# Fill by rows with a short first wait, unread products in the drain, the embedding's variance on ScalarE, one gate operation, and an end done tile by tile

## The chip, the cores and the metric

The kernel runs on one core of a Trainium2 chip. The metric is the device time of one execution in microseconds; lower is better. A core has TensorE (PE, matrix products into PSUM), VectorE (DVE), ScalarE (ACT), GpSimd (POOL) and SyncE (SP, which here only issues DMAs), each with its own instruction stream; they meet in semaphores. The profile shows TensorE's granted clock as a share of 2.4 GHz; its other level here is 1.2 GHz.

## What is computed

A small vision tower on 128 images of 64 x 64 x 3, in fp32. Patches of 16 x 16 give 16 tokens an image, 2,048 tokens of width 128.

```python
xs = concat([x, right, left, down, up])          # the image and four shifts by a pixel
y = conv(xs, conv_w, stride 16) + conv_b         # (2048 tokens, 128)
y = (y - mean(y)) * rsqrt(var(y) + 1e-3) * gamma + beta
h = y @ dense_w + dense_b
# attention without softmax, 8 heads of 16, causal decay within an image
a = layernorm(h)
scores = (q @ k.T / 4) * gammas[h] ** (j - i)    # 0 where j < i
h = h + silu(a @ wg.T + bg) * (scores @ v)
# experts: 64, top 2 of sigmoid logits, capacity 256 rows each
z = layernorm(h)
top_scores, top_idx = top_k(sigmoid(z @ gate_w.T), 2)   # weights normalised, times 2.5
routed = sum_k weight_k * (silu(rows @ w1[e]) * (rows @ w3[e])) @ w2[e]
h = h + (silu(z @ sw1) * (z @ sw3)) @ sw2 + routed
```

## The kernel before

The 2,048 tokens are 16 tiles of 128 (`NT`), in four convolution groups of four tiles (`NG`, `TG`).

**Token stage** (the loop `for i in range(LAST)` with 21 passes, written once for each engine). It is a software pipeline over tiles. Pass i of TensorE runs, in this order: a convolution product `conv_step(i, 0)`, `attend(i-3)`, `embed(i+1)`, `places(i-5)`, `scores(i-2)`, `turn(i)`, `conv_step(i, 1)`, `logits(i-4)`, `project(i-1)`. The convolution of group g+1 is spread over the passes of group g, two products of 512 columns a pass; from pass 11 on there is none left, and from pass 15 on no `embed`. I call the passes from 11 on the drain. fp32 products show as two instructions each in the profile.

DVE's pass: `decay_scores(i-3)`, `choose(i-5)`, `embedded(i)`, `gated(i-3)`, `y_stats(i+1)`, `attended(i-3)`, `accumulate(i-5)`, `place(i-5)`. `y_stats` (L798) takes mean and variance of an embedded tile, which `embed` (L423) has transposed into PSUM bank `A`; `gated` (L831) multiplies attention's output by the gate, in two operations of 64 partitions, because the two halves of the tokens lie in two PSUM banks.

ScalarE's pass: `norm_h2(i-4)`, `norm_h(i-1)`, `evac_turned(i)`, `tanhs(i-4)`, now and then `evac_y`, `evac_qk(i-1)`, `evac_vg(i-1)`. GpSimd's pass: `rstd(i)` (L1041), which gives the reciprocal deviations of three tiles that stand at different points of the pipeline, and then `send(i-6, k)` for k = 0, 1 (L1062), an indirect DMA that scatters the tile's 128 rows to the row buffer of their experts. GpSimd works in order: while a `send` waits, the next `rstd` does.

**Expert rows.** The buffer `buf` in HBM holds 256 rows (`CAP`) for each of 64 experts, then spare rows for overflow and a block of dropped rows. It has to be zero before tokens are scattered into it. `fill` is a zeroed SBUF tile of 128 partitions and 16 rows of 512 bytes (`FILLR`). SP writes it out in 8 DMAs of 1 MB (`FILLS`): the buffer is seen as 128 stretches of 128 rows, one a partition, so that each DMA writes 16 rows of each stretch, and an expert is complete only after all eight. `send(0, 0)` waits for all of them (L1067).

**SP's queue in that stage** (L298 to L347): the loads of groups 0 and 1 with the constants, a wait for the four parts of group 1 (`x_in`, L319), the drop rows, the first fill, the load of group 2 (three parts of X at 0.5 MB, one of XE at 0.38 MB that covers 96 partitions), seven more fills, the load of group 3, two fills of spare rows, then the experts' weights, paced by `y_ps`. A load of group g >= 2 waits until group g-2 has been convolved.

**Expert stage** (L599): 17 rounds of four experts: rows in by SP, four transposes, products with w1 and w3, silu on ScalarE, products on DVE, `down`, result to `buf`. It starts when all scatters have landed (L377). **Shared expert and end:** TensorE, ScalarE and DVE compute the shared expert in 8 parts; GpSimd gathers two rows a token with 32 indirect DMAs (L1097); DVE adds them to `h`, weighted, in 8 pairs of tiles (L1005): two operations for the first choice, a wait, two for the second; SP stores each pair (L397).

## Time and profile before

| | |
|---|---|
| median of 3 runs | 237.4 us (235.38 to 239.8) |
| the profiled execution | 236.28 us, of which the span of the instructions is 234.5 |
| mean granted clock of TensorE | 0.842 |
| busy: PE, DVE, POOL, ACT | 163.5, 135.6, 107.2, 83.7 us |
| DMA | 42.96 MB, 183 GB/s on average |
| chain that ended last | PE 32%, DMA 21%, POOL 14%, issue 10%, DVE 8% |

Times in the profile count from the first instruction. The chain of work that ended last is followed back from the last instruction, at each step to what released it. Its largest entry by line is GpSimd's gathers, L1097, 12%; then the DMA of the fills, 10%. The share of an engine over the whole span says little here, since the stages have different limits; each part of the change has to be read in its own stage.

### The profile page before, as it was taken

The numbers are of one execution on the slowest core, as the hardware profiler recorded it, in microseconds if no ns is written. First come the engines' busy times: TensorE is split into PE (matmuls) and PEld (weight loads), VectorE is DVE, ScalarE is ACT, GpSimd is POOL, SyncE is SP. The second block draws the span as 40 slices with busy tenths as digits, with TensorE's granted clock in tenths as the row PEclk, the third lists the DMA queues.
The fourth block names the chain that finished last, engine by engine and source line by source line (L and its number), as shares of the span: only waits on it lengthen the run. The fifth ranks groups of instructions, "written<-read, shape, count | busy, mean of one in ns | idle before, by whom it ended". The sixth has DMA issues, their size and how long they took to land.

```text
span 234.5 us, 4462 instructions
## 1 busy us (share of the span) xinstructions
PE 163.5 (70%) x1402; PEld 113.3 (48%) x1402; DVE 135.6 (58%) x487; ACT 83.7 (36%) x229; POOL 107.2 (46%) x169
## 2 busy tenths in 40 slices
PE   0888899997999987888988305999998655530000
PEld 0334455664666655656575204888887433320000
DVE  1525646684768898886447781577777422229222
ACT  2010565555256676653552202555554101100000
POOL 4004322225836666675446750133330077777760
PEclk9999999999599999975555555999999999995555
DMA  6999799999998744300000118699742612224421
GB/s 245 390 315 291 231 379 422 425 414 361 389 289 227 225 141 130 117 22 25 22 22 15 35 45 246 170 257 286 249 121 81 192 41 55 56 52 121 118 73 34
DMA packets 29213, 42.96 MB, mean 183 GB/s; under 512 B 2752, under 2 KB 21376, under 8 KB 27904
## 3 DMA queue, kind: packets, MB, share of 16 engines
q1 hardware_dynamic: 26176, 35.27, 45.0%
q0 software_dynamic: 3008, 7.34, 10.6%
q8 instruction: 13, 0.21, 0.4%
q14 instruction: 16, 0.13, 0.2%
HBM read 24.45 MB, written 18.15 MB: 182 GB/s over the span
## 4 chain that ended last, share of the span: by engine, by line
PE 32%; DMA 21%; POOL 14%; issue 10%; DVE 8%; SPq 8%; ACT 3%; POOLq 1%; DVEq 0%; ACTq 0%
POOL X L1097 12%; DMA expert_rows<-EW 10%; DMA XE<-xe 6%; PE bank L583 5%; PE scores L484 5%; PE bank L575 4%; PE scores L473 3%; PE conv_counts L419 3%; DVE go L837 2%; SPq L307 2%; DMA expert_rows<-ys 2%; PE bank L459 2%; PE bank L507 2%; POOL expert_rows L1069 2%; PE scores L596 2%
## 5 line engine op out<-in xcount | busy, mean ns | idle before, releaser
L1097 POOL DMA_INDIRECT X<-expert_rows,slots x32 | 30.6, 956 | 21.8 <-DMA expert_rows<-ys 12.3
L1069 POOL DMA_INDIRECT expert_rows<-xrow,slots x32 | 32.4, 1013 | 14.6 <-issue 8.3
L419 PE MATMUL conv_counts<-X,W 128*128 128x512 f32 x48 | 26.9, 666 | 8.0 <-DVE W L776 6.6
L688 ACT ACTIVATE qm<-bank,bqm,C 128x128 f32<-128x128 f32 x64 | 24.1, 460 | 7.0 <-PE bank L452 7.0
L484 PEld LDWEIGHTS scores<-vg,ST 64*64 64x64 f32 x512 | 19.4, 156 | 10.2 <-issue 10.2
L973 DVE TENSOR_TENSOR hT<-bank,gs 64x256 f32<-64x256 f32 x34 | 14.5, 427 | 15.1 <-ACT gs L745 14.7
L1085 POOL DMA_DIRECT2D expert_rows<-ys x12 | 9.1, 762 | 27.5 <-DVE ys L987 27.5
L484 PE MATMUL scores<-vg,ST 64*64 64x16 f32 x512 | 20.9, 222 | 0.7 <-DVE ST L884 0.2
L1054 POOL TENSOR_TENSOR VE<-MV,EPS 128x3 f32<-128x3 f32 x20 | 4.0, 199 | 36.6 <-issue 15.2
L1055 POOL TENSOR_TENSOR RS<-VE,mhalf 128x3 f32<-128x3 f32 x20 | 17.8, 889 | 1.6
L837 DVE TENSOR_TENSOR go<-scores,vg 64x128 f32<-64x128 f32 x32 | 9.1, 286 | 15.3 <-PE scores L484 15.1
L583 PE MATMUL bank<-xbT,EW 128*128 128x128 f32 x128 | 17.9, 285 | 0.0
L737 ACT ACTIVATE xbT<-bank 128x512 f32<-128x512 f32 x17 | 10.2, 597 | 20.5 <-PE bank L575 20.5
L575 PE MATMUL bank<-C,xb 128*128 128x128 f32 x68 | 11.7, 302 | 7.4 <-DMA xb<-expert_rows 7.4
L661 ACT ACTIVATE xT<-bank 128x256 f32<-128x256 f32 (+1 forms) x19 | 6.7, 351 | 28.0 <-PE bank L444 22.6
L583 PEld LDWEIGHTS bank<-xbT,EW 128*128 128x128 f32 x128 | 16.4, 200 | 0.4 <-issue 0.3
L1010 DVE SCALAR_TENSOR_TENSOR h<-X,pw,h 128x128 f32<-128x128 f32 x32 | 9.5, 349 | 11.7 <-DMA X<-expert_rows,slots 9.6
L419 PEld LDWEIGHTS conv_counts<-X,W 128*128 128x128 f32 x48 | 8.6, 212 | 15.1 <-DMA X<-xp 11.4
L473 PE MATMUL scores<-qm,kT 64*64 64x256 f32 x128 | 12.5, 462 | 4.6 <-DVE go L837 4.5
L745 ACT ACTIVATE gs<-bank 64x512 f32<-64x512 f32 x17 | 10.0, 589 | 6.7 <-PE bank L583 6.6
L575 PEld LDWEIGHTS bank<-C,xb 128*128 128x128 f32 x68 | 7.8, 150 | 9.4 <-DMA xb<-expert_rows 7.6
L1058 POOL TENSOR_SCALAR NM<-MV,RS 128x1 f32<-128x1 f32 x40 | 10.3, 271 | 4.2 <-POOL RS L1055 4.2
(129 smaller groups left out, 338.1 us busy)
## 6 DMA issues: line engine op xcount, KB each, us to landing
expert_rows<-EW SPq DMA_DIRECT2D x10, 1024.0 KB, 17.8
X<-xp SPq DMA_DIRECT2D x12, 512.0 KB, 10.8
xb<-expert_rows SPq DMA_DIRECT2D x16, 256.0 KB, 4.1
expert_rows<-ys POOLq DMA_DIRECT2D x12, 256.0 KB, 3.3
EW<-w SPq DMA_DIRECT2D x4, 512.0 KB, 4.3
EW<-wp SPq DMA_DIRECT2D x3, 640.0 KB, 6.4
XE<-xe SPq DMA_DIRECT2D x4, 384.0 KB, 13.0
expert_rows<-ys SPq DMA_DIRECT2D x4, 256.0 KB, 3.0
```

What stands on the lines that cost most here:

```text
L419: mm = nc.tensor.matmul(CONV[:, :], w, x, start=(j == 0), stop=(j == NCH + 1))
L473: mm = nc.tensor.matmul(S[toks, n, 0:QM * TB], kT[rows, t % 2, toks], qm[rows, t % 2, :, toks], start=True, stop=True)
L484: mm = nc.tensor.matmul(S[toks, c, AVC + hh * HD:AVC + (hh + 1) * HD], ST[toks, t % 2, hh], vg[toks, t % 4, hh * HD:(hh + 1) * HD], start= ...
L575: mm = nc.tensor.transpose(XT[u][:, e * BLK:(e + 1) * BLK], xb[:, v, e], ident)
L583: mm = nc.tensor.matmul(GU[u][:, e * BLK:(e + 1) * BLK], w[:, e], xbT[:, u, e], start=True, stop=True)
L688: nc.scalar.activation(qm[:, t % 2, m], QK[:, 0:P], ACT.Identity, bias=bqm[:, m:m + 1], scale=head[:, m:m + 1])
L837: ins = nc.vector.tensor_tensor(go[toks], S[toks, c, AVC:AVC + P], vg[toks, t % 4, P:2 * P], ALU.mult)
L973: ins = nc.vector.tensor_tensor(hT[a * HID:(a + 1) * HID, u], up[:, a], gate[:, a], ALU.mult)
L1055: own(pool.tensor_tensor(RS[:, b], VE[:, :], mhalf[:, :], ALU.pow))
L1058: ins = pool.tensor_scalar(NM[:, b, k:k + 1], MV[:, b, k, 0:1], RS[:, b, k:k + 1], -1.0, ALU.mult, ALU.mult)
L1069: pool.indirect_dma_start(buf, bass.IndirectOffsetOnAxis(ap=slots[:, k, t:t + 1], axis=0), xrow[:, t % XR], None).then_inc(sent[t % XR], 16)
L1097: pool.indirect_dma_start(pr[:, t, k], None, buf, bass.IndirectOffsetOnAxis(ap=slots[:, k, t:t + 1], axis=0)).then_inc(pr_in[t // TS], 16)
```

## The change

It has six parts.

1. **Fills by rows.** The buffer is now seen as 64 experts of 256 rows. A fill writes 16 rows of every expert from 64 partitions of `fill`, the lower and the upper half in turn: 16 DMAs of 0.5 MB. After eight of them the first 128 rows of every expert are zero, and more than that the first tile cannot reach. `send(0, 0)` waits for those eight, `send(1, 0)` for the rest (`filled_rest`). Group 2 is loaded after two fills (as many bytes as before). SP waits for the first two parts of group 1 only.
2. **Unread products.** Where a convolution product stood, the drain gets one of 256 columns that nobody reads, `idle_product`: two a pass from pass 11, three from pass 16, and 12 (`TURNOVER`) after the last count.
3. **Variance on ScalarE.** `embed` multiplies by `center` (the identity less 1/128) in place of transposing, so that the tile arrives without its mean; ScalarE squares it and sums (`y_variance`). DVE's `y_stats` is gone.
4. **One gate operation.** Both halves of `attend` write to the same PSUM bank, on different partitions, and `gated` is one operation of 128 partitions.
5. **End by tiles.** DVE adds a tile's two rows in two dependent operations, tile after tile; SP stores pairs, but the last two tiles one by one.
6. The semaphores that go with these (`pr_in` for each tile).

```diff
-        FILLS = NE * CAP // P // FILLR
+        FILLS = CAP // FILLR
+        FIRST_FILLS = P // FILLR
+        TURNOVER = 12
@@ sync
-            for part in range(NL + 1):
+            for part in range(NL - 1):
                 sp.wait_ge(x_in[1][part], 16)
-            main = buf[0:NE * CAP].rearrange("(p r) w -> p r w", p=P)
+            main = buf[0:NE * CAP].rearrange("(e r) w -> e r w", e=NE)
             for n in range(FILLS):
-                if n == 1:
+                if n == 2:
                     load_group(2)
-                sp.dma_start(main[:, n * FILLR:(n + 1) * FILLR], fill[:, :, :]).then_inc(filled, 16)
+                half = slice(n % 2 * NE, (n % 2 + 1) * NE)
+                sp.dma_start(main[:, n * FILLR:(n + 1) * FILLR], fill[half]
+                             ).then_inc(filled if n < FIRST_FILLS else filled_rest, 16)
@@ sync, the stores
-            for p in range(NS):
-                sp.wait_ge(fin_ready, p + 1)
-                sp.dma_start(ov[:, p * TS:(p + 1) * TS], h[:, p * TS:(p + 1) * TS]).then_inc(stored, 16)
+            ends = list(range(TS, NT, TS)) + list(range(NT - TS + 1, NT + 1))
+            for first, end in zip([0] + ends, ends):
+                sp.wait_ge(fin_ready, end)
+                sp.dma_start(ov[:, first:end], h[:, first:end]).then_inc(stored, 16)
@@ tensor
-                nc.tensor.transpose(A[:, 0:P], y, ident)
+                nc.tensor.matmul(A[:, 0:P], y, center, start=True, stop=True)
-                        mm = nc.tensor.matmul(S[toks, c, AVC + hh * HD:AVC + (hh + 1) * HD], ST[toks, t % 2, hh],
+                        mm = nc.tensor.matmul(S[toks, 0, AVC + hh * HD:AVC + (hh + 1) * HD], ST[toks, t % 2, hh],
+            def idle_product(i, n):
+                if i == NT - TG - 1 and n == 0:
+                    pe.wait_ge(yT_ready, NG)
+                nc.tensor.matmul(CONV[:, 0:2 * P], W[:, 0], W[:, 1:3], start=True, stop=True)
             def conv_step(i, n):
                 g, j = (i + 1) // TG + 1, 2 * ((i + 1) % TG) + n
+                if g >= NG:
+                    return idle_product(i, n)
@@ tensor, in the loop, after places(i - 5), and after the last count
+                if i >= NT:
+                    idle_product(i, 2)
+            for n in range(TURNOVER):
+                idle_product(LAST, n)
@@ scalar
+            def y_variance(t):
+                act.wait_ge(y_ps, t + 1)
+                nc.scalar.activation(ysq[:, :], A[:, 0:P], ACT.Square, scale=P ** -0.5,
+                                     accum_out=MV[:, t % 2, 0, 1:2]).then_inc(ystat, 1)
                 if 0 <= i - 1 < NT:
                     norm_h(i - 1)
+                if i + 1 < NT:
+                    y_variance(i + 1)
@@ vector
-                for c in range(NTB):
-                    toks = slice(c * TB, (c + 1) * TB)
-                    ins = nc.vector.tensor_tensor(go[toks], S[toks, c, AVC:AVC + P], vg[toks, t % 4, P:2 * P], ALU.mult)
-                ins.then_inc(av_read, 1)
+                nc.vector.tensor_tensor(go[:, :], S[:, 0, AVC:AVC + P], vg[:, t % 4, P:2 * P], ALU.mult
+                                        ).then_inc(av_read, 1)
-                if i + 1 < NT:
-                    y_stats(i + 1)
+            for t in range(NT):
+                dve.wait_ge(pr_in[t], 16 * TOPK)
+                dve.wait_ge(so_ready, t // TS + 1)
                 for k in range(TOPK):
+                    ins = nc.vector.scalar_tensor_tensor(out=h[:, t], in0=pr[:, t, k], scalar=pw[:, t, k:k + 1],
+                                                         in1=h[:, t], op0=ALU.mult, op1=ALU.add)
                     if k < TOPK - 1:
+                        own(ins)
                 ins.then_inc(fin_ready, 1)
@@ gpsimd, send(t, k)
                 if t == 0:
-                    pool.wait_ge(filled, 16 * FILLS)
+                    pool.wait_ge(filled, 16 * FIRST_FILLS)
                     pool.wait_ge(drop_filled, 16)
+                if t == 1:
+                    pool.wait_ge(filled_rest, 16 * (FILLS - FIRST_FILLS))
```

## Rows read from the trace of the kernel before

**Rows 1.** The page's slices: granted clock of TensorE, tenths, 40 slices.

```profile
PEclk9999999999599999975555555999999999995555
```

**Rows 2.** Chain that ended last, in order of time: start, us, what.

```profile
30.91 22.66 DMA expert_rows<-EW
...
143.22 1.97 PE bank L575 x8
```

**Rows 3.** Timeline of GpSimd: start, us, line and work, idle time before.

```profile
48.69 0.51 POOL L1058 TENSOR_SCALAR NM<-MV,RS 128x1 f32<-128x1 f32 x2 [0.21 <-POOL RS L1055]
54.61 1.23 POOL L1069 DMA_INDIRECT expert_rows<-xrow,slots  x1 [5.42 <-DVE slots L863]
...
129.30 0.22 POOL L1054 TENSOR_TENSOR VE<-MV,EPS 128x3 f32<-128x3 f32 x1 [0.69 <-DVE MV L849]
```

**Rows 4.** Timeline of TensorE: attends of passes 6, 8, 11, 15, 18, and others.

```profile
49.81 1.11 PE L484 MATMUL scores<-vg,ST 64*64 64x16 f32 x32
...
54.89 1.13 PE L419 MATMUL conv_counts<-X,W 128*128 128x512 f32 x2
...
58.88 0.45 PE L429 MATMUL bank<-C,yT 128*128 128x128 f32 x1 [1.82 <-DVE h L871]
...
66.19 1.11 PE L484 MATMUL scores<-vg,ST 64*64 64x16 f32 x32
...
76.27 0.60 PE L459 MATMUL bank<-SQ,xT 128*128 128x256 f32 x2
76.70 0.27 PE L460 MATMUL bank<-bvg,ones 96*128 96x256 bf16 x1
...
82.78 1.11 PE L484 MATMUL scores<-vg,ST 64*64 64x16 f32 x32
...
105.15 1.89 PE L484 MATMUL scores<-vg,ST 64*64 64x16 f32 x32
...
125.76 1.89 PE L484 MATMUL scores<-vg,ST 64*64 64x16 f32 x32 [0.24 <-DVE ST L884]
...
135.55 0.27 PE L567 MATMUL conv_counts<-acc,ones 128*128 128x64 bf16 x2 [0.47 <-DVE mpos L856]
```

**Rows 5.** Busy time by stretch, clock, DMA share, GB/s: XE loads; fills alone.

```profile
20.50:22.50 2.00, 2.00 (x8) 1.02 (x7) 1.65 (x7) 0.00 (x0) 0.72 (x4) 1.00 1.01 209
31.90:33.40 1.50, 1.50 (x24) 0.74 (x24) 0.00 (x0) 1.50 (x7) 0.00 (x0) 1.00 0.89 273
36.00:50.00 14.00, 13.52 (x137) 8.61 (x137) 9.81 (x39) 8.43 (x27) 4.77 (x12) 1.00 1.01 423
55.50:57.00 1.50, 1.50 (x34) 1.01 (x32) 0.00 (x0) 1.09 (x5) 1.20 (x2) 1.00 1.09 243
```

**Rows 6.** The same for two drain steps: length, PE, PEld, DVE, ACT, POOL, clock.

```profile
88.10:93.43 5.33, 4.26 (x58) 3.08 (x59) 4.80 (x22) 3.47 (x12) 3.61 (x7) 1.00 0.44 133
105.10:112.65 7.55, 6.62 (x56) 4.58 (x55) 4.45 (x19) 3.47 (x12) 4.53 (x8) 0.50 0.09 27
```

**Rows 7.** Timeline of DVE: gate and y_stats in a drain step; the end.

```profile
84.28 0.57 DVE L837 TENSOR_TENSOR go<-scores,vg 64x128 f32<-64x128 f32 x2
84.88 0.30 DVE L803 BATCH_NORM_STATS2 stats<-bank 128x6 f32<-128x128 f32 x1
85.21 0.18 DVE L805 BATCH_NORM_AGGREGATE MV<-stats 128x2 f32<-128x6 f32 x1
...
229.44 1.26 DVE L1010 SCALAR_TENSOR_TENSOR h<-X,pw,h 128x128 f32<-128x128 f32 x4 [3.57 <-DMA X<-expert_rows,slots]
```

**Rows 8.** Timeline of ScalarE in a drain step.

```profile
91.40 0.38 ACT L661 ACTIVATE xT<-bank 128x256 f32<-128x256 f32 x1 [1.06 <-PE bank L444]
```

**Rows 9.** Issue to landing: fill 0 (24.32), XE of group 2 (27.36), X of group 3 (31.44).

```profile
DMA to landing us min/median/max: 5.1/5.1/5.1
...
DMA to landing us min/median/max: 7.7/7.7/7.7
...
DMA to landing us min/median/max: 23.4/24.7/26.2
```

More of the change, by code:

```diff
@@ L168, in tower @@
         go = sb("go", [P, P])
+        ysq = sb("ysq", [P, P])
         xrow = sb("xrow", [P, XR, P])
@@ L225, in tower @@
         filled_tile, filled = sem("filled_tile"), sem("filled")
-        spare_filled, drop_filled = sem("spare_filled"), sem("drop_filled")
+        filled_rest, spare_filled, drop_filled = sem("filled_rest"), sem("spare_filled"), sem("drop_filled")
         ones_set = sem("ones_set")
@@ L252, in tower @@
             "sh_ps", "shg_ready", "shT_ready", "so_ps", "so_ready"))
-        pr_in = [sem(f"pr_in{n}") for n in range(NS)]
+        pr_in = [sem(f"pr_in{n}") for n in range(NT)]
         fin_ready, stored = sem("fin_ready"), sem("stored")
@@ L287, in turns @@
             return min(max(i - FIRST2 + 1, 0), LAST2 - FIRST2 + 1)
-        FILLS = NE * CAP // P // FILLR
+        FILLS = CAP // FILLR
+        FIRST_FILLS = P // FILLR
         SPARES = NOV * BLK // P // FILLR
         PACE = 6
-        assert FILLS * FILLR * P == NE * CAP and SPARES * FILLR * P == NOV * BLK
+        TURNOVER = 12
+        assert FILLS * FILLR == CAP and SPARES * FILLR * P == NOV * BLK
         def first_blocks(g):
@@ L340, in load_weights @@
                 sp.wait_ge(w_ready, NL)
-                sp.wait_ge(filled, 16 * FILLS)
+                sp.wait_ge(filled, 16 * FIRST_FILLS)
+                sp.wait_ge(filled_rest, 16 * (FILLS - FIRST_FILLS))
                 sp.wait_ge(spare_filled, 16 * SPARES)
@@ L396, in _ @@
             ov = out.rearrange("(t p) d -> p t d", p=P)
-            for p in range(NS):
-                sp.wait_ge(fin_ready, p + 1)
-                sp.dma_start(ov[:, p * TS:(p + 1) * TS], h[:, p * TS:(p + 1) * TS]).then_inc(stored, 16)
-            sp.wait_ge(stored, 16 * NS)
+            ends = list(range(TS, NT, TS)) + list(range(NT - TS + 1, NT + 1))
+            for first, end in zip([0] + ends, ends):
+                sp.wait_ge(fin_ready, end)
+                sp.dma_start(ov[:, first:end], h[:, first:end]).then_inc(stored, 16)
+            sp.wait_ge(stored, 16 * len(ends))
         @block.tensor
@@ L717, in _ @@
             nc.scalar.activation(WD[:, :], QK[:, 0:P], ACT.Copy).then_inc(wd_ready, 1)
+            y_variance(0)
             for i in range(LAST):
@@ L796, in step @@
                 return steps[0]
-            def y_stats(t):
-                dve.wait_ge(y_ps, t + 1)
-                if t == 0:
-                    dve.wait_ge(ones_set, 1)
-                s = step(nc.vector.bn_stats(stats[:, 0], A[:, 0:P]))
-                dve.wait_ge(dve_step, s)
-                nc.vector.bn_aggr(MV[:, t % 2, 0], stats[:, 0]).then_inc(ystat, 1)
             def choose(t):
@@ L909, in split_bias @@
                 ins.then_inc(bvg_ready, 1)
-            y_stats(0)
             for i in range(LAST):
@@ L1003, in _ @@
                     evac_out(n + NB, 0)
-            for p in range(NS):
-                dve.wait_ge(pr_in[p], 16 * TOPK * TS)
-                dve.wait_ge(so_ready, p + 1)
+            for t in range(NT):
+                dve.wait_ge(pr_in[t], 16 * TOPK)
+                dve.wait_ge(so_ready, t // TS + 1)
                 for k in range(TOPK):
-                    for t in range(p * TS, (p + 1) * TS):
-                        ins = nc.vector.scalar_tensor_tensor(out=h[:, t], in0=pr[:, t, k], scalar=pw[:, t, k:k + 1],
-                                                             in1=h[:, t], op0=ALU.mult, op1=ALU.add)
-                        if k < TOPK - 1:
-                            last = step(ins)
+                    ins = nc.vector.scalar_tensor_tensor(out=h[:, t], in0=pr[:, t, k], scalar=pw[:, t, k:k + 1],
+                                                         in1=h[:, t], op0=ALU.mult, op1=ALU.add)
                     if k < TOPK - 1:
-                        dve.wait_ge(dve_step, last)
+                        own(ins)
                 ins.then_inc(fin_ready, 1)
@@ L1098, in _ @@
                         pr[:, t, k], None, buf,
-                        bass.IndirectOffsetOnAxis(ap=slots[:, k, t:t + 1], axis=0)).then_inc(pr_in[t // TS], 16)
+                        bass.IndirectOffsetOnAxis(ap=slots[:, k, t:t + 1], axis=0)).then_inc(pr_in[t], 16)
 def kernel(x, L0_tok_conv_w, L0_tok_conv_b, L0_tok_gamma, L0_tok_beta, L0_tok_dense_w, L0_tok_dense_b,
```

3 lines of the change are left out of this document (1 added, 2 removed).

## The prediction

> **What bounds the kernel now.** I read the page first, then the chain that ended last, then the timelines of the engines on it. The slices show the granted clock of TensorE: a slice is 5.86 us, and it is full up to the 10th, half in the 11th (from 58.6), full again, and half from the 19th to the 25th (105.5 to 146.6) [rows 1]. So three things are to be placed: a stall near 55 us, a slow drain of the token stage from about 100 us on, and the end. Step i of the token stage means pass i of its loop; I know a pass by its `attend`, the 32 small products of L484.
>
> The chain passes through one long DMA: the last fill of the expert rows, issued at 30.91 and landed 22.66 us later, at 53.6 [rows 2]. GpSimd's first scatter waits for it: GpSimd was done with its statistics at 49.2 and starts the scatter at 54.61 [rows 3]. It issues in order, so the next `rstd` is late, DVE's `embedded` with it, and TensorE starts the embedding of step 7 only at 58.88; the attend of step 8 starts at 66.19 [rows 4]. Later, over the four steps from 82.78 to 105.15, a step costs 5.6 us, over the three from 105.15 to 125.76 it is 6.9 [rows 4]. In one step of the first stretch DVE is busy 4.80 of 5.33 us and TensorE 4.26; in one of the second TensorE, at half clock, is busy 6.62 of 7.55 and DVE only 4.45 [rows 6]. So DVE bounds the drain at 2.4 GHz and TensorE at 1.2 GHz. The clock fell some 20 us after the last convolution product (which lies before the attend at 82.78), in steps in which the engine was busy 80% of the time. After that: the expert stage (TensorE starts on the rows that have landed at 143.22 [rows 2]), and gathers on GpSimd with one DVE group of four behind the last [rows 7].
>
> **Fills.** Before, 8 DMAs of 1 MB read all 128 partitions of `fill`; after, 16 of 0.5 MB read 64 each, the two halves in turn. Bytes are the same, 8.39 MB. All SP loads go through one queue and land in order, so what counts is the whole queue: drop rows, fills, group 2, fills, group 3. Three dates come from rows. Fill 0 landed at 29.4 (24.32 + 5.1) and XE of group 2 at 35.1 (27.36 + 7.7), so group 2 takes 5.7 us. The first X part of group 3 landed at 54.85 (31.44 + 23.4), 1.3 after the last fill [rows 9]. TensorE starts the first product on it at 54.89 [rows 4]: this data is just in time, and it stays behind all the fills. SP no longer waits for the last two parts of group 1, so the queue runs on without the gap in which SP issued: I let the fills begin at 23.7. Group 3's first part then lands at 23.7 + 8.39 MB / rate + 5.7 + 1.3.
>
> The rate is the unknown that decides. Between 36 and 50 us, fills alone, the queue moved 423 GB/s at a DMA share of 1.01. But while the XE load of group 1, 2 or 3, which covers 96 partitions, is in transit, the share stays near one and the bytes fall: 209, 273 and 243 GB/s [rows 5]. The engines are then busy and yet slow, so a transfer over fewer partitions is slower in this trace. No row shows 64 partitions in bulk. Lower bound 209, upper bound 423; the mean of the three XE stretches is 242, and 64 is further down than 96, so I take the middle between that and 209, 225 GB/s. Then the fills take 37.3 us and group 3 begins to land at 68.0.
>
> The Trainium skill bears on this. "SBUF — State Buffer", section on the DMA port swizzle, says that partitions 0 to 63 reach only 8 of the 16 ports, about 218 GB/s instead of 436, and that two DMAs in flight, one on each half, were only 6% quicker than one. By it the fills take 38.5 us and the sum below comes to 238.7; by the row of 423 GB/s it comes to 220.3. The rule speaks against the change, and the three XE rows agree with its direction.
>
> What waits then? The first wait, for 8 of the 16 fills (4.2 MB, 18.6 us, plus group 2), ends at about 48.4, before GpSimd is free at 49.2: it is hidden. The new wait of scatter 1 for the rest ends at about 67. Behind it on GpSimd stand `rstd(8)`, then `embedded(8)`, and all of the next step. TensorE waits meanwhile itself, for X of group 3. After 68.0 it does that product (1.7 at half clock: 512 columns, four times the 0.43 found below for 256) and the attend (1.9), so the embedding of step 7 starts at about 71.7 and the attend of step 8 some 6.8 later, at 78.5 (before: 7.3 later, six of them at half clock). Against 66.19 that is **+12.3 us**. The 8 more issues on SP (0.46 each) lie in its waits; the weight loads behind them are not used before 143. If the fills run at 423, the data lands at 50.5, the stall goes and with it its price. That price: the attends of steps 6 and 8 lie 16.38 apart, and two undisturbed steps take 2 x 5.8 (the three from 66.19 to 82.78, 16.59, plus the 0.86 of convolution that the last of them lacks), so **4.7 us**.
>
> **Drain.** Per step DVE loses `y_stats` (0.30 + 0.18) and one of the two gate operations (0.57 for two, so 0.29) [rows 7]: about 0.7. TensorE gets two products of 256 columns; one such pair takes 0.43, from 76.27 to 76.70 [rows 4]. It also gets a second pass for `center` (0.06). 4.26 + 0.86 + 0.06 is 5.2: TensorE becomes the bound, the step goes from 5.6 to 5.15 on average, **-1.8** over four. The variance on ScalarE stands where that engine idles 1.06 before L661 [rows 8]. A 128-column activation with a sum isn't in the trace; it costs between nothing and that row's 0.38 for 256 columns and twice that, all of it under the idle time. The wait of the first product for the last `evac_y` is met by then.
>
> With the fillers TensorE is busy nearly all of a step, as it was while the convolution ran and the clock stayed full. So I let it hold 2.4 GHz. The three steps from 105.15 then cost 3.3 (half of 6.62) + 0.9 to 1.3 of fillers; GpSimd and DVE allow no less than about 4.5 [rows 6], so 4.5 + 4.8 + 4.5 against 20.6: **-6.8**. From the last attend to the `rstd` that starts GpSimd's closing run it is 3.5 now (125.76 to 129.30 [rows 3]) and 2.3 with a 1.1 us attend: **-1.2**. The run itself is scatters and keeps its length. The 12 closing products take 5.1 us behind the last count (135.55 now [rows 4]), 7.7 before the rows are there, so they end some 2.5 early; whether the clock is still full then is open: between 0 and 1.5 (the first eight transposes take 1.97 at half clock [rows 2], a product group as much after them), I take **-0.7**.
>
> **End.** After the last gather DVE runs four operations in 1.26 [rows 7]; after, two dependent ones, 0.73. The last store is 64 KB instead of 128: **-0.6** together, bounds 0.4 and 0.9. One more store costs SP half a microsecond before the last data is there.
>
> **Sum.** +12.3 - 1.8 - 6.8 - 1.2 - 0.7 - 0.6 = +1.2. The profiled execution took 236.28 (span 234.5 and 1.8 around it), so 237.5. The median of the three runs is 237.4, between 235.38 and 239.8: no change.
>
> **Rivals.** (1) The fills keep 423 GB/s because the halves alternate and the engines drift apart: -4.7 - 11.1 - 0.2 for an earlier start gives 220.3. For it: ordinary fills never slow down after 36 us, and the XE penalty varies (209 to 273). Against it: at 20.5 every engine was slow at once. Above 258 GB/s the result is faster by over 2%. (2) Slower: the clock is not held. Then each filler costs 0.86 instead of 0.43. The three steps take 8.4, 9.3 and 7.0 (+4.1), the tail +1, and twelve closing products need 10.3 where 7.7 are free (+2.6); with the rest, +5.3 in place of -11.1, so 254. It decides once half of the drain runs at 1.2 GHz. For it: the clock fell at 80% busy; against: the fillers close just those gaps. (3) The fills run below 200 GB/s, more than two engines on one port: each 10 GB/s less costs 2 us; at 170 it is 249. (4) The drain is bound by the chain through ScalarE and GpSimd and gives half: 242.
>
> **Chances.** Forecast 0.50 (its own range 232 to 243), (1) 0.30, (2) 0.08, (3) 0.07, (4) 0.05. Within 2% (about what a measurement of this kernel can tell): 0.42 of the forecast and 0.03 of (4), 0.45. Faster: (1) and 0.04 of the forecast, 0.34. Slower: (2), (3), 0.02 of (4), 0.04 of the forecast, 0.21. The range must take in (1), so 218 to 243; it leaves out (2), most of (3) and little else.
>
> **What would show it.** The stretch 36 to 60 near 225 GB/s with the DMA share at one; the 16th fill landing near 67; GpSimd waiting some 12 us before its third scatter; TensorE waiting as long at L419 for X; the attend of step 8 near 78; from there no half clock; steps of 5.2 and then 4.5 to 4.8; DVE idle in the drain. Wrong it is if the 36 to 50 stretch still moves over 400, or if slices of half clock remain in the drain.

## The result and the profile after

The changed kernel took 223.37 us (median of four runs, 222.13 to 224.05) against 236.59 of the kernel before on the same chip (235.38 to 239.8): ratio 0.945, 95% interval 0.938 to 0.953. It is faster; the forecast was 237.5 and no change. Of the profiled execution the span is 220.3 us, before 234.5.

On the chips of the experiments the kernel before took 226 to 242 us, at a mean granted clock from 0.91 down to 0.81. Its one trace (0.842) has the half clock in the drain; that it is this stretch which differs from execution to execution is likely, but only that one trace was kept. So most of what follows compares intervals within traces. The ratios to before in the sections below are taken among executions within some 1.5% of the fastest of each kernel, so they can differ from the quotient of the medians.

The slices of the changed kernel (clock and what the DMA engines moved) stand beside [rows 1]: the stall in the 11th slice and the half clock of the drain are gone.

```profile
PEclk9999999999999999999999997999999999985555
DMA  6999999999999984510000168799534412124530
```

The stretch of fills alone as in [rows 5], and one drain step as in [rows 6] (length, PE, PEld, DVE, ACT, POOL, clock, DMA share, GB/s):

```profile
36.00:50.00 14.00, 14.00 (x158) 9.26 (x156) 8.38 (x33) 9.70 (x34) 5.37 (x12) 1.00 1.01 419
88.59:93.74 5.15, 5.11 (x64) 3.76 (x63) 4.25 (x19) 3.73 (x14) 3.61 (x7) 1.00 0.46 130
```

The fills alone, 64 partitions each, moved 419 GB/s where 225 was forecast; over 400 in this stretch was the prediction's own sign of being wrong. Timeline of GpSimd, as [rows 3]: its first scatter now starts at 48.56 (54.61 before), behind its own work and no fill, and the `rstd` that starts its closing run at 116.25 (129.30).

```profile
48.56 1.23 POOL L1081 DMA_INDIRECT expert_rows<-xrow,slots  x1 [0.52 <-issue]
...
54.05 1.07 POOL L1081 DMA_INDIRECT expert_rows<-xrow,slots  x1 [0.29 <-issue]
...
116.25 0.21 POOL L1064 TENSOR_TENSOR VE<-MV,EPS 128x3 f32<-128x3 f32 x1
```

Timeline of TensorE, as [rows 4]: the attends of passes 6, 8, 11, 15 and 18, the product on X of group 3 between the first two, and the idle products behind the count.

```profile
49.27 1.11 PE L491 MATMUL scores<-vg,ST 64*64 64x16 f32 x32
54.80 1.12 PE L426 MATMUL conv_counts<-X,W 128*128 128x512 f32 x2 [0.62 <-DMA X<-xp]
...
61.54 1.11 PE L491 MATMUL scores<-vg,ST 64*64 64x16 f32 x32
...
78.31 1.11 PE L491 MATMUL scores<-vg,ST 64*64 64x16 f32 x32
...
98.89 1.11 PE L491 MATMUL scores<-vg,ST 64*64 64x16 f32 x32
...
113.25 1.11 PE L491 MATMUL scores<-vg,ST 64*64 64x16 f32 x32 [0.31 <-DVE ST L900]
...
122.40 5.43 PE L548 MATMUL conv_counts<-W 128*128 128x256 f32 x24
130.14 0.66 PE L593 MATMUL bank<-C,xb 128*128 128x128 f32 x4 [2.32 <-DMA xb<-expert_rows]
```

Stage by stage, from attend to attend of the passes named, the change of the span comes out whole:

| stretch | before | after | change | forecast |
|---|---|---|---|---|
| start to attend of pass 8 | 66.19 | 61.54 | -4.65 | +12.3 |
| to pass 11 | 16.59 | 16.77 | +0.18 | 0 |
| four steps, to pass 15 | 22.37 | 20.58 | -1.79 | -1.8 |
| three steps, to pass 18 | 20.61 | 14.36 | -6.25 | -6.8 |
| to the `rstd` that starts the closing run | 3.54 | 3.00 | -0.54 | -1.2 |
| to the first gather | 58.60 | 57.66 | -0.94 | -0.7 |
| to the last gather | 39.09 | 38.88 | -0.21 | 0 |
| to the end of the span | 7.48 | 7.48 | 0.00 | -0.6 |

### The profile page after: what moved, and what is told of

It is laid out like the page before. It is cut to its first block, busy times and chain, and to the rows that moved or that the text cites. A ratio compares the mean times of both kernels' runs of the same rounds, so it can differ in the third digit from the quotient of the medians.

```text
span 220.3 us, 4641 instructions
## 1 busy us (share of the span) xinstructions
PE 168.2 (76%) x1492; PEld 118.2 (54%) x1492; DVE 125.6 (57%) x439; ACT 88.8 (40%) x261; POOL 106.6 (48%) x169
## 4 chain that ended last, share of the span: by engine, by line
PE 42%; POOL 16%; DMA 16%; SPq 13%; issue 9%; DVE 1%; POOLq 1%; ACT 0%; DVEq 0%
POOL X L1109 13%; DMA X<-xp 11%; PE bank L601 8%; SPq L332 7%; PE scores L491 5%; PE bank L593 4%; PE conv_counts L426 3%; PE conv_counts L548 3%; SPq L310 3%; PE scores L480 3%; PE scores L614 3%; PE conv_counts L614 2%; PE bank L466 2%; POOL expert_rows L1081 2%; PE bank L436 2%
## 5 line engine op out<-in xcount | busy, mean ns | idle before, releaser
L491 PEld LDWEIGHTS scores<-vg,ST 64*64 64x64 f32 x512 | 16.2, 134 | 9.1 <-issue 8.3
L548 PE MATMUL conv_counts<-W 128*128 128x256 f32 x74 | 20.7, 390 | 0.0
L764 ACT ACTIVATE xbT<-bank 128x512 f32<-128x512 f32 x17 | 10.2, 597 | 20.1 <-PE bank L593 20.1
L491 PE MATMUL scores<-vg,ST 64*64 64x16 f32 x512 | 17.7, 207 | 0.3 <-DVE ST L900 0.3
L1022 DVE SCALAR_TENSOR_TENSOR h<-X,pw,h 128x128 f32<-128x128 f32 x32 | 10.3, 351 | 9.5 <-DMA X<-expert_rows,slots 6.7
L853 DVE TENSOR_TENSOR go<-scores,vg 128x128 f32<-128x128 f32 x16 | 4.7, 292 | 15.2 <-PE scores L491 15.2
L548 PEld LDWEIGHTS conv_counts<-W 128*128 128x128 f32 x74 | 12.2, 192 | 1.6 <-ACT yT L662 0.2
L734 ACT ACTIVATE shg<-conv_counts 128x256 f32<-128x256 f32 x8 | 3.1, 384 | 23.7 <-PE conv_counts L525 23.7
L900 DVE TENSOR_TENSOR ST<-scores,C 128x512 f32<-128x512 f32 x16 | 11.1, 692 | 1.9 <-PE scores L480 1.9
## 6 DMA issues: line engine op xcount, KB each, us to landing
X<-xp SPq DMA_DIRECT2D x12, 512.0 KB, 10.5
```

What stands on the lines that cost most here:

```text
L491: mm = nc.tensor.matmul(S[toks, 0, AVC + hh * HD:AVC + (hh + 1) * HD], ST[toks, t % 2, hh], vg[toks, t % 4, hh * HD:(hh + 1) * HD], start= ...
L548: nc.tensor.matmul(CONV[:, 0:2 * P], W[:, 0], W[:, 1:3], start=True, stop=True)
L900: nc.vector.tensor_tensor(ST[:, t % 2].rearrange("p (n m) i -> p n (m i)", m=QM), S[:, :, 0:QM * TB], decay.rearrange("p (n f) -> p n f", ...
```

## The fills: which partitions, which order, which wait

**e1_lower_half.** All fills read the same 64 partitions.

```
-                half = slice(n % 2 * NE, (n % 2 + 1) * NE)
+                half = slice(0, NE)
```

> The changed kernel with one edit: all 16 fills read partitions 0 to 63 of the zero tile; before this edit they took the lower and the upper half in turn. Bytes, rows written and number of transfers stay. Theory A (64 partitions are slow by themselves, and only the alternation of halves, with several transfers in flight, hid it): the fills move about 218 GB/s, 38 us instead of 20, the first X part of group 3 lands near 69 instead of 54.8, TensorE waits some 14 us for it, and the time is about 223.4 + 15 = 238. Theory B (how many partitions a fill reads does not matter for its rate): over 400 GB/s between 36 and 50, X at 54.8, time 223 to 224.

**e2_half_blocks.** `half = slice(n // 8 * NE, (n // 8 + 1) * NE)`.

> The changed kernel with one edit: the first eight fills read partitions 0 to 63, the last eight partitions 64 to 127, so neighbours in the queue read the same half. Theory A: as slow as with the lower half alone, 236 to 238, since only the two fills at the change of halves overlap. Theory B: 223 to 224, over 400 GB/s.

Measured: 242.57 us (242.21 to 243.85) and 242.97 (241.59 to 243.87), some 5 us more than either theory A expected; ratio to before on that chip 1.072 for both (the medians, 232.27 before, give 1.04 and 1.05). The unedited changed kernel took 222.5 on that chip. The windows of the first, then of the second (columns as above):

```profile
42.00:50.00 8.00, 8.00 (x86) 5.24 (x84) 5.81 (x25) 5.70 (x19) 3.27 (x8) 1.00 1.00 208
57.00:66.00 9.00, 0.00 (x0) 0.00 (x0) 0.00 (x0) 0.11 (x1) 0.00 (x0) 0.63 1.00 213
```

```profile
42.00:50.00 8.00, 8.00 (x90) 5.24 (x91) 5.80 (x25) 5.86 (x21) 3.29 (x7) 1.00 0.99 221
57.00:66.00 9.00, 0.00 (x0) 0.00 (x0) 0.00 (x0) 0.00 (x0) 0.00 (x0) 0.55 0.98 222
```

Theory A holds. Fills of 64 partitions run at half the rate, 208 to 222 GB/s, with the DMA share still at one, when their neighbours in the queue read the same half; with the halves in turn they run at 419. In the trace's packet records an 8 KB packet takes 636 to 638 ns (medians) in the first case and 309 in the second. In e1 X of group 3 lands at 70.85 (expected 69), TensorE stands still from 54.6 to 70.9, and the clock is half from 59.4 to 79.9, so that the attend of pass 8 comes at 81.78, 20.2 us later than in the changed kernel. That half clock, under which TensorE works for the last 9 us of it, was in neither theory and fits the 5 us on top.

**e3_old_fills.** The fills, the waits for them and SP's full wait as before, all else as changed. Of its edit, the line of the fill:

```
-                sp.dma_start(main[:, n * FILLR:(n + 1) * FILLR], fill[half]
-                             ).then_inc(filled if n < FIRST_FILLS else filled_rest, 16)
+                sp.dma_start(main[:, n * FILLR:(n + 1) * FILLR], fill[:, :, :]).then_inc(filled, 16)
```

> The changed kernel with the fills as before: 8 transfers of 1 MB from all 128 partitions, the scatter of the first tile waits for all of them, and SP waits for all four parts of group 1 first. Everything else stays. If the hidden first wait is worth what the stall cost before (4.7 us between the attends of passes 6 and 8), the attend of pass 8 is again near 66.2 and the time is 223.4 + 4.7 = 228. If TensorE's wait for X of group 3 had been the true end of that stall, no more than 1 us: 224.

**e11_long_first_wait.** The fills stay, the first scatter waits for all of them.

```
                 if t == 0:
                     pool.wait_ge(filled, 16 * FIRST_FILLS)
+                    pool.wait_ge(filled_rest, 16 * (FILLS - FIRST_FILLS))
```

> The changed kernel, but the first scatter waits for all 16 fills, not for the first eight. The fills stay by rows, half a tile each, in the same order. Theory (the short first wait is what removes the stall; earlier issue and smaller transfers bring nothing): scatter 0 at 54 instead of 48.6, attend of pass 8 near 66 with the clock at half behind it, 223 + 4.7 = 227.5, as with the old fills. Rival (the earlier start of the fills has a part in it): 224 to 226.

Measured: 228.01 (226.46 to 228.77) with the old fills, as expected; scatter 0 at 54.81, attend of pass 8 at 66.61. With the long first wait alone 226.79 (224.97 to 229.87; the unedited changed kernel did not run on that chip), scatter 0 at 53.88, the clock half for 3.4 us where it was half for 6.8, and the attend of pass 8 at 64.28, where 66 was expected. Against 61.54 the old fills cost 5.07 us up to that attend, the long first wait alone 2.74. So the short first wait is more than half of what takes the stall away. The other 2.3 us go with a first scatter 0.9 earlier and the shorter stretch at half clock; whether other executions divide alike no trace shows.

**e7_full_wait.** `range(NL - 1)` is `range(NL + 1)` again, so SP starts the fills later.

> The changed kernel with SP's wait for all four parts of group 1 ahead of the fills again, so that they start 3 us later, as before (23.9 instead of 20.9). Everything behind stays. In the trace of the changed kernel X of group 3 landed at 54.75, where it landed before (54.85), so the earlier start seems to have been lost between 20.5 and 28, where 222 to 234 GB/s were moved. Theory (the earlier start brings nothing): X of group 3 lands within 0.7 us of 54.8 and the time is that of the changed kernel, 222 to 229. Rival (it brings its 3 us): X lands near 57.5, TensorE waits 3 us, the clock falls at 57, and no execution is under 226.

Measured: 232.46 (226.07 to 233.82); before on that chip 232.02 (the unedited changed kernel did not run there, v2 of the next section took 223.25). My theory fell and the rival holds. The fills were issued from 23.12, 1.8 us later than in the changed kernel, X of group 3 landed at 56.4, and TensorE waited for it:

```profile
56.41 1.80 PE L426 MATMUL conv_counts<-X,W 128*128 128x512 f32 x2 [2.07 <-DMA X<-xp]
```

The clock fell at 56.7 for 6.8 us, and the attend of pass 8 came at 66.23. The halves in turn have a price at the start of the queue. Windows of the kernel before and of the changed one:

```profile
25.00:28.00 3.00, 2.88 (x15) 1.96 (x16) 1.42 (x6) 1.18 (x4) 1.43 (x4) 1.00 1.00 318
```

```profile
25.00:28.00 3.00, 3.00 (x17) 2.00 (x16) 0.85 (x4) 1.82 (x7) 1.56 (x4) 1.00 0.97 234
```

In both the first fills are in transit there, beside loads of X. The first 1 MB of fills landed 5.1 us after its issue before and in e3; in two halves it took 6.8 in e7, which starts behind the same wait, and 7.0 in the changed kernel. By the landing of XE of group 2 the loss has grown to 2.6 to 2.9 us (10.8 us behind the issue of the first fill before, 13.4 in e7, 13.7 in the changed kernel), and in the fills that follow nothing more is lost. Why the start is slower is not shown. The earlier start, 21.28 instead of 24.32, pays for that loss, so that X of group 3 lands at 54.75 as it did before; without it every execution was 226 or more.

## When X of group 3 lands

**v2_x_ahead.** The first part of group 3 goes ahead of the last two fills (and is left out of `load_group(3)`).

```
+                if n == FILLS - 2:
+                    sp.wait_ge(conv_ps, 2)
+                    sp.dma_start(X[:, 1, 0:HC], xp[3, :, 0:HC]).then_inc(x_in[1][0], 16)
```

> The changed kernel with one edit: the first X part of group 3 is loaded ahead of the last two fills. In profiled executions of kernels with the part behind the fills TensorE waited 0.46, 0.62, 1.71, 2.33, 2.94 and 3.45 us for it, and in those with more than 1.7 the clock fell to half near 57.5 for 3.4 to 10.2 us. Theory (that wait is what makes the changed kernel differ by 8 us between executions): no wait for X at L426 above 0.3 us, no half clock near 57, all executions between 221.5 and 223.5. Rival (the clock falls there for another reason): executions near 227 to 230 remain.

Measured: 223.25 (220.1 to 224.06), all six executions within 4 us, where 2 were expected, at a mean clock of 0.934 to 0.942, and none near 227. The product no longer waits:

```profile
54.53 1.10 PE L429 MATMUL conv_counts<-X,W 128*128 128x512 f32 x2
```

There is a price: the last fill now lands at 57.69, the scatter of the second tile waits 4.3 us for it (58.49 instead of 54.05), and the attend of pass 9 comes at 67.23, as in the changed kernel (67.24). So where X had been in time the edit gains nothing there; what it takes away are the slow executions.

Most of the changed kernel's spread is probably that of this landing. Of its three profiled executions the two with waits of 0.46 and 0.62 us took 222.44 and 222.13; in the third, a2 below, 228.69, TensorE waited 2.94 us for X and the clock was half from 57.85 for 6.8. The product on X after a wait of 2.33 us (the kernel with one early product, below) is followed by an attend at half clock, 1.81 us instead of 1.11:

```profile
56.32 1.13 PE L426 MATMUL conv_counts<-X,W 128*128 128x512 f32 x2 [2.33 <-DMA X<-xp]
57.38 1.81 PE L491 MATMUL scores<-vg,ST 64*64 64x16 f32 x32
```

and the attend of pass 8 comes at 66.19 there, 4.65 us later than at 61.54. Waits of 0.46 to 1.29 in other traces had no such fall behind them, but for those of e3 (1.15) and e11 (0.76), in which the stall of the late first scatter stands close behind; one of 1.71 had one of 3.4 us.

## The drain: products, DVE, places

**e4_no_products.** No idle product anywhere (the matmul in `idle_product` is left out).

> The changed kernel without any of the idle products, in the drain and behind the count alike; variance on ScalarE, one gate operation and the fills stay. Theory of the prediction (the products hold the clock): the clock falls to half near pass 15, the three attends from pass 15 to 18 take some 20 us again instead of 14.4, the tail 1 us more, the steps before the fall 5.0 or less instead of 5.15: 223.4 + 6 to 7 = 230. Rival (DVE's relief made the drain faster and the clock would have held, or does not matter): 223 to 225.

Measured: 224.69 (220.91 to 229.0); the executions differ by 8 us. In the profiled one, 220.91, the clock held until 110.0 and was half for 23.9 us. The expected times were wrong: at full clock a step took 4.70 us, not 5.0, and the three attends from pass 15 to 18 took 13.68, not some 20, because the clock held 33 us behind the last convolution product (75.9 to 76.9), where it had held 21 in the kernel before. Slices of this execution, and its product of the logits in a step at full clock:

```profile
PEclk9999999999999999999955557999999999985555
```

```profile
90.96 0.43 PE L514 MATMUL bank<-SQ,xT 128*128 128x64 f32 x2 [0.47 <-ACT xT L684]
```

TensorE waits 0.47 us for ScalarE ahead of the logits there. So the products cost 0.44 us in a full step, 2.24 over the seven steps from pass 11 to 18 (34.94 in the changed kernel, 32.70 here). What they seem to buy is that the clock doesn't fall early: 222.5 with them (five of six within 221.5 to 224.3, one 227.68), on the same chip 220.91, 221.67, 227.72 and 229.0 without. The mean clock was 0.89 in the two short ones and 0.86 in the two long ones, of which no trace was kept. The profiled one also shows that DVE's relief alone can bring the fast drain, without any product.

**e10_one_product.** Only the product ahead of the attend (`n == 0`); **v1_late_product** only the one ahead of the logits.

```
                 if g >= NG:
-                    return idle_product(i, n)
+                    return idle_product(i, n) if n == 0 else None
```

> The changed kernel with one idle product a step in the drain instead of two (the one ahead of the attend; the one ahead of the logits is left out). Without any, a step took 4.70 us at 2.4 GHz until the clock fell at 109.99; with two it took 5.14 and the clock stayed. Theory A (one is enough to hold the clock): steps of 4.92, 7 x 0.22 = 1.5 us faster than the changed kernel, clock full to the expert stage. Theory B (it isn't): the clock falls to half between passes 15 and 18, as without any, and the time is 0 to 6 us above the changed kernel, differing from execution to execution.

> The changed kernel with one idle product a step in the drain again, but the other one: the product ahead of the attend is left out, the one ahead of the logits stays. The trace without products shows TensorE idle 0.69 us ahead of the logits (it waits there for ScalarE's copy of the transposed rows) and no idle time ahead of the attend; with one product ahead of the attend a step still took 5.14. Theory A (the product ahead of the attend is the whole price, the other one is free, and one holds the clock until the expert stage): steps of 4.70 to 4.75, 2.8 us faster than the changed kernel (222.5 on this chip), about 219.7. Theory B (a product a step is no cover): the clock falls in the drain as without any, at 110 or earlier, and the time is 221 to 229, differing from execution to execution. Theory C (any product costs its 0.22): 221.5.

Measured: e10 225.18 (222.81 to 226.08), v1 220.66 (218.94 to 223.75). With the one product ahead of the attend the seven steps from pass 11 to 18 take 34.93 us (82.96 to 117.89), as with two (34.94); neither of its theories said that. The clock held over these steps, and was half from 118.95 to 129.19. With the one ahead of the logits the seven steps take 32.68, as without any (32.70), and theory A holds for the price: the product in TensorE's wait for ScalarE is free, the one ahead of the attend is the whole 0.44. For the clock it holds only in part, in v1 it was half from 117.4 to 124.2, behind the last attend at 111.04. The unedited changed kernel did not run on v1's chip, so its 220.66 has no neighbour there.

**e8_dve_undone.** `y_stats` with its two operations and the gate in two halves are back on DVE.

> The changed kernel with DVE's part undone: the variance of the embedding is again two DVE operations (0.30 and 0.18 us) behind the transposing product, and the gate is again two operations of 64 partitions (0.57 together). Idle products, fills and end stay. Theory (with the products DVE and TensorE would both bind a drain step, DVE at 5.3 to 5.6): the eight steps of the drain take 5.5 instead of 5.14, +2.5 to 3.5 us over the changed kernel. Rival (TensorE with its products is the bound and covers 0.75 us of DVE work): less than 0.8 us slower.

Measured: 225.94 (223.72 to 227.65), on the chip where the changed kernel took 222.5. From the attend of pass 3 to that of pass 18 it took 83.16 us against 80.32: +2.8, of which 1.6 lie in the drain (steps of 5.33) and 1.3 in the steps with convolution (5.79 against 5.69). The first theory holds in size, but not in place: its steps of 5.5 were 5.33, and that DVE also binds a little while the convolution runs was not in it. In this run the clock stayed full through the whole drain, until 135.7, so the idle products hold it without DVE's relief too.

## The closing products

**e5_no_closing.** `TURNOVER = 0`; **e6_closing18** has 18.

> The changed kernel without the 12 closing products behind the count; the products of the drain stay. In the changed kernel the clock fell to half 1.8 us after the expert transposes began, for 3.4 us, and the first down product came 5.47 us after the transposes began against 5.60 before. Theory (the closing products gave nothing, 0.1 us at most): same time as the changed kernel within 0.5 us. Rival (the prediction: they let the expert stage start at full clock, 0.7): 0.7 to 1.5 us slower, because the clock falls while TensorE idles for 8 us and stays half over the first groups.

> The changed kernel with 18 closing products instead of 12. Twelve end 2.3 us before the expert rows are there, and the clock fell to half 1.8 us after the expert transposes began; from the last scatter to the first store of expert results it is 13.2 to 13.4 us, where kernels whose clock was full in that stretch took 11.7 to 11.9. Theory (the idle stretch ahead of the rows causes the fall): the clock stays full into the expert stage, 1.4 us faster than the changed kernel. Rival (the fall comes from what TensorE does in the expert stage's first groups, or the six further products delay it): same time, or 0.3 us slower.

Measured: e5 223.08 (221.9 to 224.98), with 12 of them 222.5 on that chip. From the last scatter to the first store of expert results it is 13.62 us without and 13.19 with, but from the last scatter to the first gather 49.28 without and 50.37 with. So they are worth about half a microsecond at most, between the two theories, and nearer the first. e6 took 225.79 (220.98 to 228.66), the unedited kernel 226.34 on that chip; in the profiled execution, 228.66, X of group 3 landed late (TensorE waited 3.45). Within its trace the clock stayed full from 67.5 to 204, and from the last scatter to the first gather it took 48.47 us, against 49.04 and 50.37 in two traces with twelve, which differ by more than the gain in question; to the first store 12.30 against 13.36 and 13.19. That points to a gain of 1 us; one trace doesn't show it.

Other traces bear on the rival. Where the clock was full in the first expert groups, the first down product came 4.79 (e6), 4.31 (e10) and 4.25 us (v1 and both v3) behind the first transpose, with twelve closing products in all but e6; in the traces in which the clock fell in the stage it came after 5.32 to 5.57 (changed kernel 5.47), without closing products (e5) after 5.82. So a full clock there goes with 0.7 to 1.2 us less. In e10, v1 and v3 the clock had fallen behind the drain and risen again before the expert rows landed. The twelve products of the changed kernel leave TensorE idle for 2.3 us just ahead of the stage.

## The end

**e9_end_undone.** Additions and stores by pairs of tiles again.

> The changed kernel with the end by pairs of tiles again: DVE waits for the gathers of two tiles and adds them in four operations, SP stores 128 KB at a time, eight stores. Theory of the prediction (the last tile alone is done sooner): 0.4 to 0.9 us slower than the changed kernel. Rival (nothing is gained: from the start of the last gather to the end of the span it is 7.51 us in the trace before and 7.47 in that after): same time within 0.3 us.

**x2_last_store_later.** Four operations more ahead of the last store.

```
+                if t == NT - 1:
+                    own(ins)
+                    for _ in range(3):
+                        own(nc.vector.tensor_scalar(go[:, :], go[:, :], 1.0, None, ALU.mult))
+                    ins = nc.vector.tensor_scalar(go[:, :], go[:, :], 1.0, None, ALU.mult)
                 ins.then_inc(fin_ready, 1)
```

> The changed kernel with four more DVE operations on a scratch tile (0.3 us each) between the last addition and the last store. Theory (GpSimd's drain behind its last gather ends the program: it ended 7.24 us after the last gather began in both traces, the last store had landed at 217.7 of 220.3 in the changed kernel): the last store lands 1.4 us later, near 219.1, and the interval from the last gather to the end of the span stays 7.5. Theory of the prediction (the last store ends it): 1.4 us longer, 8.9.

Measured: e9 226.77 (221.59 to 229.64) and x2 227.02 (221.96 to 230.99); X of group 3 landed late in both, so their totals say nothing on the end. From the start of the last gather to the end of the span it is 7.47 us in e9 and 7.48 in x2, in the changed kernel and before. In x2 the last store landed at 222.45 of 223.96, in the changed kernel at 217.71 of 220.26: 1 us later by the last gather (5.96 behind its start instead of 4.92), and the end did not move. What ends last is GpSimd's drain. The line of the block's end, before, changed and x2 (min, median and max in ns, start in us):

```profile
L102 POOLq DRAIN  x1: 21420/21420/21420, 212.8 to 212.8; - x1
```

```profile
L102 POOLq DRAIN  x1: 21317/21317/21317, 198.7 to 198.7; - x1
```

```profile
L102 POOLq DRAIN  x1: 21508/21508/21508, 202.2 to 202.2; - x1
```

It ends at 234.2, 220.0 and 223.7, 7.24 us after the last gather began, and so it does in all twenty traces. The second theory, that of the prediction, has fallen.

## The changed kernel again, and a faster one

**a1_changed_again, a2_changed_again.** Unedited, on two other chips.

> The changed kernel once more, unedited, as the measure for the other kernels on this chip: 223.4, between 222.1 and 224.1, if it repeats what it did. On another chip the kernel before took 226 to 234 instead of 235 to 240, so it is open whether the changed one moves as well. If the idle products remove the early fall of the clock, its spread stays about 2 us while that of the kernel before is 8.

> The changed kernel, unedited, as the measure for the three others on this chip: 222 to 224. Some executions near 227, in which TensorE gets X of group 3 over a microsecond later and the clock falls near 57.

**v3_late_and_x_ahead, v3_again.** v1 and v2 together, on two chips.

> The kernel of v1 with the first X part of group 3 loaded ahead of the last two fills instead of behind them. In the changed kernel TensorE waits 0.46 to 0.62 us for it, and in the kernel with one product ahead of the attend it waited 2.33 and the clock then fell to half for 6.8 us. Theory (that wait and the fall behind it are gone): X lands 2.4 us earlier, near 52.3; the last fill lands 1.3 later, near 54.5, where GpSimd wants to start the scatter of the second tile at 54.05; 0.5 us faster than v1 in the median, and no execution with a fall near 57. Rival (the scatter of the second tile waits instead, and its rstd is late): no gain, or 0.5 us slower.

> The kernel with one idle product a step, ahead of the logits, and the first X part of group 3 loaded ahead of the last two fills, again and beside the changed kernel on one chip. If its 219.35 against 222.5 to 223.4 is no matter of the chip: 3.5 to 4.5 us faster than the changed kernel, of which 2.8 come from the steps of 4.7 and 0.6 from TensorE's wait for X.

Measured: a1 222.5 (221.48 to 227.68), before 232.86 there, ratio 0.960 (0.953 to 0.966). a2 226.34 (223.43 to 230.48), ratio 0.988 (0.980 to 0.996), before 231.74 there. v3 219.35 (217.1 to 221.88); beside a2, on its chip, 217.72 (216.71 to 218.72), ratio to before 0.961 (0.953 to 0.969). So the gain of the change isn't 5.5% everywhere, it was 1 to 4% there (4.4 and 2.3% by the medians), and a2's median missed the expected 222 to 224. v3 beats both kernels: its slowest execution beside a2 is 4.7 us under a2's fastest, and the medians lie 8.6 apart, more than the 3.5 to 4.5 expected; in a2's profiled execution X had landed late. Between profiled executions (spans of 216.6 and 215.3 against the 220.3 of the changed kernel) it is 3.7 to 5.0. The 5.0 divide into 1.1 up to the attend of pass 8, 0.6 to pass 11, 2.3 to pass 18 and 1.0 between the last scatter and the first gather. The rival of v3 came true, the scatter of the second tile waits until 56.73 for the last fill, but it cost nothing: the attend of pass 9 comes 5.70 us behind that of pass 8, as in the changed kernel. In v3_late_and_x_ahead the clock was half from 115.8 to 122.6 and full from there to the last slices.

## Why the prediction was wrong, and where it was right

**Fills, +12.3: wrong, and it decides.** The step that failed is "I take the middle between that and 209, 225 GB/s". The rate was 419, and what happened is rival (1) with its 220.3 (profiled execution 222.13). The two bounds of that step were the two real cases: 208 to 222 with neighbours on one half, 419 with the halves in turn (that the lower bound, read from loads over 96 partitions, met the first is luck). I had the sentence for it, "the halves alternate and the engines drift apart", and gave it 0.30. What misled me was to read the slow XE stretches of [rows 5] as a mean rate for a kind of transfer, and to apply it to a queue in which neighbours complement each other. With the 213 GB/s of e1, the formula gives 23.7 + 39.4 + 7.0 = 70.1 for X of group 3; it landed at 70.85, and the attend of pass 8 came 10.9 us behind it, 10.5 by the prediction. The path through the kernel was right, the rate was not. But the 70.1 is right by luck, since the formula is too short: with the 423 of before it gives 26.8 us from the issue of the first fill to X of group 3, where 30.5 are in the trace of before (the first fill took 5.1 us for 1 MB, 2.5 at that rate, and the last seven moved 397 GB/s). In e1 a start 2.4 us earlier than the assumed 23.7 makes up for most of that. (The prediction's 48.4 for the end of the first wait adds up to 48.0, 23.7 + 18.6 + 5.7, which changes nothing.) "SBUF — State Buffer" of the Trainium skill says in its section on the DMA port swizzle that 64 partitions reach about 218 GB/s: the traces of e1 and e2 agree (208 to 222). With what it says under "Can I just issue two DMAs to hit both halves?", that two in flight are only 6% quicker than one, the traces differ: in this queue of sixteen it is 419 against 213. The measurement decides.

**The stall's price, -4.7: right in the sum, by luck in part.** -4.65 was measured up to the attend of pass 8, and e3 gives it back, e11 2.74 of it. But the prediction's 4.7 is priced between the attends of passes 6 and 8, where 16.38 became 12.27, so 4.1; the other 0.54 were gained before pass 6. From the attend of pass 3 to that of pass 6 it took 17.03 us before, 16.51 in the changed kernel, and 17.03 again in e8: that is DVE's relief, which the prediction counted in the drain alone. **The earlier start, -0.2: wrong in what it is worth.** It was 3.0 us, not 0.2, it moved no landing, but without it (e7) the fills land too late.

**What was missing: the margin of X of group 3.** The prediction called this data "just in time" [rows 4] and went no further; by its short formula it even had the data at 50.5 in the case of 423 GB/s, and it landed at 54.75. A microsecond or two more and the clock falls.

**Drain, -1.8 and -6.8: right in size, -1.79 and -6.25.** "TensorE becomes the bound" is half right: a product ahead of the attend lies on the path, one ahead of the logits doesn't, and the sum of busy times (5.2) met the 5.14 by accident, which is 4.70 and the 0.44 of one product. That the clock holds was right in every trace with two products a step, with and without DVE's relief (e8); that it needs them was not shown, since it also held until 110.0 in e4. The tail's -1.2 was -0.54: the attend got 0.8 shorter, and what takes up the rest is open (v1, with one product fewer, has 3.15 us there, the changed kernel 3.00).

**Closing products, -0.7: nearly nothing at the start of the expert stage.** The first down product came 5.47 us after the transposes began, 5.60 before; the clock fell in the stage instead of being half at its start. The -0.94 of this stretch lies mostly (-0.78) between GpSimd's last store of expert results and the first gather, where SP issues the last eight (12.32 against 13.10); no run takes this apart.

**End, -0.6: wrong.** DVE's 1.26 did become 0.74, and the last store landed 0.6 us sooner behind the start of the last gather (4.92 against 5.55), but the sum took the last store for the end. The span of before, 234.5, lay 2 us behind that store; the prediction didn't ask what fills them.

## What to carry to other kernels

When a rate is disputed between two bounds a factor of two apart, ask what stands next in the queue: it is the mix of neighbours that decides, and the middle is the one value that occurs in neither case. Try a formula on the kernel before, where the answer is known: here that would have shown 3.7 us missing. Look for the transfer that arrives just in time, put it ahead of what can wait, and do it before anything else: here a landing 1.5 us later (e10) put the attend of pass 8 back by 4.65. Work that is put in to keep an engine busy belongs where that engine waits anyway; and at the end, look which engine's drain ends last before making the last store quicker.

## What the runs showed of the hardware

- 64-partition transfers out of SBUF share a limit: 8 KB packets took 636 to 638 ns (medians) with neighbours in the queue on one half, 208 to 222 GB/s, and 309 ns with the halves in turn, 419 GB/s, the DMA share at one in both.
- At the start of the queue the halves in turn were slower than transfers over 128 partitions: 6.8 to 7.0 us for the first 1 MB against 5.1.
- GpSimd's drain at the end of the program ended 7.24 us after its last gather began in all twenty traces, whatever the stores did.
- TensorE fell from 2.4 to 1.2 GHz behind single waits of 1.7 to 3.5 us in a busy stretch, for 3.4 to 10.2 us (behind waits of 15.7 and 16.3 in e2 and e1, for 20.5), and not behind those of 0.46 to 1.29, but for e3 and e11. In the drain without idle products it fell at 110.0, 33 us after the last convolution product, in the kernel before at 102.5, 21 us after it. What tells these apart stays open.
